# Attention probabilities turned in 32x32 squares by VectorE and exchanged through DRAM, in place of TensorE transposes

## The reference, cut to what matters

```
# layer 1
s = jnp.einsum('bhqe,bhke->bhqk', q, k) * scale
s = jnp.where(mask, s, jnp.finfo(s.dtype).min)
p = jax.nn.softmax(s, axis=-1)
o = jnp.einsum('bhqk,bhke->bhqe', p, v)
# layer 2
attn = jnp.einsum('bqc,bkc->bqk', q * scale, k)
attn = attn + rel_h[:, :, :, :, None] + rel_w[:, :, :, None, :]
attn = jax.nn.softmax(attn, axis=-1)
out = attn @ v
```

## Time and profile before

| | |
|---|---|
| median of 3 runs | 1289.74 us (1288.63 to 1292.06) |
| the profiled execution | 1289.51 us, span 1287.5 us |
| PE busy | 1256.3 us, 98% of the span |
| DVE / ACT / POOL busy | 631.2 / 537.7 / 641.0 us |
| mean granted TensorE clock | 0.998 of full speed |
| DMA | 96.33 MB, mean 75 GB/s |

### The profile page before, as it was taken

The page is one execution under the profiler, slowest core; times in us unless marked ns, Lnnn a source line. Parts: engine busy times, 40 slices in busy tenths (PEclk is TensorE's granted clock), DMA queues, the critical chain, the costliest instruction groups (busy, mean ns, idle before and its releaser), DMA issues.

```text
span 1287.5 us, 19996 instructions
## 1 busy us (share of the span) xinstructions
PE 1256.3 (98%) x7216; PEld 1018.3 (79%) x7216; DVE 631.2 (49%) x1323; ACT 537.7 (42%) x1357; POOL 641.0 (50%) x726
## 2 busy tenths in 40 slices
PE   6999998999999999999999999999999999999998
PEld 4887894478888888888888888888888887778787
DVE  7533453774444233545243465754436656666212
ACT  3612140045656430656452066564305665543212
POOL 4633299055454556555546655455565554564000
PEclk9999999999999999999999999999999999999999
DMA  5211123022222233222233323233333233220011
GB/s 179 86 44 42 43 55 103 8 70 75 67 82 67 81 80 95 74 75 75 74 81 97 97 81 95 80 90 86 91 91 93 82 93 81 73 74 1 17 50 66
DMA packets 83297, 96.33 MB, mean 75 GB/s; under 512 B 24960, under 2 KB 46112, under 8 KB 83200
## 3 DMA queue, kind: packets, MB, share of 16 engines
q1 hardware_dynamic: 82048, 92.97, 25.4%
q10 hardware_dynamic: 1152, 2.10, 0.5%
HBM read 82.45 MB, written 8.39 MB: 71 GB/s over the span
## 4 chain that ended last, share of the span: by engine, by line
PE 88%; DVE 5%; issue 2%; ACT 2%; SPq 1%; DMA 0%; POOL 0%; ACTq 0%; DVEq 0%; POOLq 0%
PE PS L1126 53%; PE PS L680 6%; PE PS L1762 5%; PE PS L1194 4%; PE PS L1171 4%; PE PS L945 3%; PE PS L1210 2%; PE PS L960 2%; PE PS L1220 2%; PE PS L1779 2%; PE PS L1240 1%; SPq L1027 1%; PE PS L663 1%; PE PS L954 1%; PE PS L1186 1%
## 5 line engine op out<-in xcount | busy, mean ns | idle before, releaser
L1126 PE MATMUL PS<-XB,w_hi 128*128 128x512 f32 x1024 | 358.3, 403 | 1.4 <-POOL w_lo L227 1.2
L225 POOL CAST w_hi<-w_raw 128x512 fp32r<-128x512 f32 x195 | 124.9, 640 | 327.6 <-PE PS L1126 254.8
L227 POOL TENSOR_TENSOR w_lo<-w_raw,w_hi 128x512 fp32r<-128x512 f32 x195 | 253.7, 1301 | 15.6
L1126 PEld LDWEIGHTS PS<-XB,w_hi 128*128 128x128 f32 x1024 | 192.3, 188 | 41.8 <-issue 2.4
L1126 PE MATMUL PS<-XB,w_lo 128*128 128x512 f32 x512 | 200.0, 391 | 0.0
L1126 PE MATMUL PS<-XB,part 128*128 128x512 f32 x768 | 198.9, 397 | 0.0
L1126 PEld LDWEIGHTS PS<-XB,part 128*128 128x128 f32 x768 | 140.1, 188 | 27.8
L1404 ACT ACTIVATE part<-PS,nmax 128x256 f32<-128x256 f32 (+1 forms) x256 | 112.4, 447 | 64.4 <-DVE nmax L1529 44.7
L1421 ACT ACTIVATE part<-PS 128x384 f32<-128x384 f32 (+1 forms) x128 | 69.6, 544 | 135.1 <-PE PS L1194 134.9
L225 POOL CAST part<-part 128x512 fp32r<-128x512 f32 x85 | 55.8, 656 | 122.3 <-PE PS L1126 121.6
L227 POOL TENSOR_TENSOR part<-part,part 128x512 fp32r<-128x512 f32 x85 | 111.2, 1308 | 6.8
(11 more groups left out here) (140 smaller groups left out, 1986.4 us busy)
## 6 DMA issues: line engine op xcount, KB each, us to landing
w_raw<-in_w SPq DMA_DIRECT2D x187, 256.0 KB, 2.7
part<-in_w SPq DMA_DIRECT2D x85, 256.0 KB, 2.7
strips<-part SPq DMA_DIRECT2D x16, 256.0 KB, 3.3
out_x<-xT SPq DMA_DIRECT2D x16, 256.0 KB, 2.1
part<-strips SPq DMA_DIRECT2D x128, 24.0 KB
xT<-in_x ACTq DMA_DIRECT2D x8, 256.0 KB, 7.6
xT<-in_x SPq DMA_DIRECT2D x8, 256.0 KB, 9.8
w_raw<-in_w SPq DMA_DIRECT2D x16, 128.0 KB, 3.4
```

The costliest lines, as they stand in the source:

```text
L225: pool.tensor_copy(hi, raw).then_inc(w_hi_done, 1)
L227: pool.tensor_tensor(lo, raw, hi.bitcast(F32), ALU.subtract).then_inc(w_ready, 1)
L1126: m = nc.tensor.matmul(PS[:, bank, :], wt[:, (c % 4) * P:(c % 4) * P + P], rhs(hl, c), start=c == k == 0, stop=c == CK - 1 and k == 2)
```

## The change

The PE transposes of probabilities and their copies by ACT go. DVE turns each tile of probabilities in 32x32 squares (`turn_probs`, now a VectorE function) into `probB`. The squares still have to change places among the four groups of 32 partitions: SP writes them to the DRAM tensor `turned` (four transfers for a batch a of an item, 128 pieces each) and reads them back into `probT` (one transfer for each a). `PROBS_AT` says behind which weight half block that is issued. `attend(i)` waits for the reads and stands behind `scores(i + 1)`; its right operand is read from the squares by a four-part pattern. Probabilities have two buffers instead of four, and score banks are free when the exponentials are taken.

Beside it: V's blocks are loaded ahead of the output blocks; Q goes to bank X, `turn_values` to a score bank; the strips are written from ACT's queue; K's scale of layer 2 is applied where relative positions are added, so K's evacuation has one DVE operation instead of two; the lambda part's shifts for t = 0 are issued by ACT, and its key groups are ordered so that those that need t = 0 come later; in layer 0 two of four evacuations of Q go ahead of the copies of windows; at the end the normalization of the last half is done in three portions around the evacuations of the first product.

```diff
             if i + 1 < ITEMS:
                 take_block(i + 1, "K")
+            take_block(i, "V", range(0 if i else 1, 2))
             if s and j == 0:
                 for o in range(CK):
                     take((s - 1, "O", o), STAGES[s - 1][0], "O", o)
-            take_block(i, "V", range(0 if i else 1, 2))
             if i + 2 < ITEMS:
...
         for jp in range(2):
             for b in (2 * jp, 2 * jp + 1):
                 exp_k(b)
+            evac_q(jp, range(2))
             if jp:
                 in_between()
-            evac_q(jp)
+            evac_q(jp, range(2, 4))
...
-    prob = carve(13824, [P, 4, 2, N])
+    prob = carve(13824, [P, 2, 2 * N])
+    probB = [carve(at, [P, 4 * N]) for at in (14848, 11264)]
...
-    probT = carve(16384, [P, 4, HALF])
+    probT = carve(16384, [P, 2, 4 * N])
+    turned = nc.dram_tensor("turned", (2, 2, P, 4 * N), F32).ap()
...
+    def add_keys_groups(b, mc):
+        groups.extend(("K", (b, mc, nh)) for nh in range(2))
+
+    def add_y_groups(b):
+        groups.extend(("Y", (b, nh, vt)) for nh in range(2) for vt in range(2))
+
+
+    KEYS = [(0, 1), (1, 1), (0, 0), (1, 0), (2, 1), (2, 0)]
+    for b, mc in KEYS:
+        add_keys_groups(b, mc)
+    add_y_groups(0)
+    for mc in (1, 0):
+        add_keys_groups(3, mc)
+    for b in range(1, B):
+        add_y_groups(b)
...
+    def shift(eng, t):
+        evacuated(eng, max(i for i, (kind, d) in enumerate(groups) if kind == "G" and d[0] == t))
+        for src, y, dst, mc in shifts(t):
+            eng.dma_start(A2[dst, mc, y, :, :].rearrange("p x g -> p (x g)"), G[t][src, y - rows_of[t][0], :])\
+                .then_inc(shifted[t], 16)
...
         copy_windows(act, range(2, len(quads)))
+        shift(act, 0)
...
-        for t in rows_of:
-            evacuated(sp, max(i for i, (kind, d) in enumerate(groups) if kind == "G" and d[0] == t))
-            for src, y, dst, mc in shifts(t):
-                sp.dma_start(A2[dst, mc, y, :, :].rearrange("p x g -> p (x g)"), G[t][src, y - rows_of[t][0], :])\
-                    .then_inc(shifted[t], 16)
+        for t in (3, 1, 2):
...
+    def squares(i):
+
+        return 4 if layer_of(i) == 2 else 3
+
+    def prob_at(i, qt):
+
+        return sum(hi - lo for lo, hi in spans(i)[:qt])
...
-                pe.wait_ge(t_evac, 4 * (i - 1) + 2 * a + 2)
+                pe.wait_ge(p_exp, 4 * (i - 1) + 2 * a + 2)
+                if a == 0 and turned_bank(i - 1) == S:
+                    pe.wait_ge(v_ready, i)
...
-        def turn_probs(i, k):
-
-            n = 4 * i + k
-            pe.wait_ge(p_norm, n + 1)
-            for kt_, qt, at in tiles(i):
-                m = nc.tensor.transpose(PS[:, S + k, at:at + P], prob[:, k, qt, kt_ * P:kt_ * P + P], ident[:, :])
-            m.then_inc(t_done, 1)
...
         def attend(i, a):
-            pe.wait_ge(t_evac, 4 * i + 2 * a + 2)
+            pe.wait_ge(p_in[a], 16 * (i + 1))
...
+            n = squares(i)
+
+            turned_p = probT[:, a, 0:8 * P * n // 4].rearrange("p (q h s j) -> p q h s j", q=4, h=2, s=n)
             if layer_of(i) == 2:
                 for kt_ in range(2):
                     for hh in range(2):
+                        rhs = turned_p[:, :, hh, kt_::2, :].rearrange("p q s j -> p s q j")
                         m = nc.tensor.matmul(PS[64 * hh:64 * hh + 64, O, a * N:a * N + N],
-                                             v[:, 2 * a + kt_, 64 * hh:64 * hh + 64],
...
-        def attention_block(i):
-
-            if i:
-                attend(i - 1, 0)
-                attend(i - 1, 1)
+        def score_block(i):
+
             scores(i, 0)
             scores(i, 1)
             relative(i + 1)
...
         for i in range(1, LAST - 1):
-            attention_block(i)
-            project(i + 1, "K", range(0, 6))
-            turn_probs(i, 0)
-            project(i + 1, "K", range(6, CK))
+            score_block(i)
+            attend(i - 1, 0)
+            attend(i - 1, 1)
+            project(i + 1, "K", range(CK))
+            project(i, "V", range(CK))
             if i % PAIRS == 0:
                 s = i // PAIRS - 1
                 out_block(s, 0, range(0, 2))
-                turn_probs(i, 1)
-                out_block(s, 0, range(2, 7))
-                turn_probs(i, 2)
-                out_block(s, 0, range(7, CK))
-                out_block(s, 1, range(0, 3))
-                turn_probs(i, 3)
-                out_block(s, 1, range(3, CK))
-                for o in range(2, CK):
+                turn_values(i)
+                out_block(s, 0, range(2, CK))
+                for o in range(1, CK):
                     out_block(s, o, range(CK))
-                project(i, "V", range(CK))
+                project(i + 2, "Q", range(CK))
+            else:
                 project(i + 2, "Q", range(0, 2))
                 turn_values(i)
                 project(i + 2, "Q", range(2, CK))
-            else:
-                project(i, "V", range(0, 2))
-                turn_probs(i, 1)
-                project(i, "V", range(2, 7))
-                turn_probs(i, 2)
-                project(i, "V", range(7, CK))
-                project(i + 2, "Q", range(0, 2))
-                turn_values(i)
-                project(i + 2, "Q", range(2, 3))
-                turn_probs(i, 3)
-                project(i + 2, "Q", range(3, CK))
...
+        attend(LAST, 0)
+        attend(LAST, 1)
+        for o in range(3):
+            out_block(3, o, range(7, CK))
+            for k in M_AFTER[o, 1]:
...
-            if n >= 4:
-                act.wait_ge(t_done, n - 3)
+            if n >= 2:
+                act.wait_ge(t_done, n - 1)
             for qt, (lo, hi) in enumerate(spans(i)):
-                last = nc.scalar.activation(prob[:, k, qt, lo:hi], PS[:, S + k, qt * N + lo:qt * N + hi],
+                at = prob_at(i, qt)
+                last = nc.scalar.activation(prob[:, n % 2, at:at + hi - lo], PS[:, S + k, qt * N + lo:qt * N + hi],
...
-        def evac_t(i, k):
-            n, w = 4 * i + k, P * len(tiles(i))
-            act.wait_ge(t_done, n + 1)
-            if i:
-                act.wait_ge(o_done, 2 * i)
-            nc.scalar.activation(probT[:, k, 0:w], PS[:, S + k, 0:w], ACT.Copy).then_inc(t_evac, 1)
...
+            strips_to_dram(act, i)
...
             exps(i, 0)
-            evac_relative(i + 1)
             exps(i, 1)
             normalize(i, 0)
             normalize(i, 1)
-            evac_t(i, 0)
+            evac_relative(i + 1)
             exps(i, 2)
             normalize(i, 2)
-            if i < LAST:
-                evac_k(i + 1)
-            else:
-                evac_v(i)
-            evac_t(i, 1)
             exps(i, 3)
+            if i and j == 0:
+                evac_o(i - 1)
             normalize(i, 3)
-            evac_t(i, 2)
-            out_between = i and i % PAIRS == 0
-            if i < LAST and not out_between:
-                evac_v(i)
-            evac_t(i, 3)
-            if out_between:
-                evac_v(i)
-            if 1 <= i % PAIRS <= 4:
-                for c in (2 * (i % PAIRS) - 2, 2 * (i % PAIRS) - 1):
-                    norm.y(nc.scalar, i // PAIRS + 1, c)
-                for c in (2 * (i % PAIRS) - 2, 2 * (i % PAIRS) - 1):
-                    norm.head(i // PAIRS + 1, c)
+            evac_k(i + 1)
+            if j:
+                evac_o(i - 1)
+            evac_v(i)
...
-                nc.vector.tensor_tensor(scores, scores, both_rel[:, n % 2, :, :, :].rearrange("p a h w -> p (a h w)"), ALU.add)\
-                    .then_inc(rel_added, 1)
+                nc.vector.scalar_tensor_tensor(scores, scores, SCALE, both_rel[:, n % 2, :, :, :].rearrange("p a h w -> p (a h w)"),
+                                               ALU.mult, ALU.add).then_inc(rel_added, 1)
...
+        def turn_probs(i, k):
+
+            n, a, hh, m = 4 * i + k, k // 2, k % 2, squares(i)
+            dve.wait_ge(p_norm, n + 1)
+            if i:
+                dve.wait_ge(p_out[a], 64 * i)
+            src = prob[:, n % 2, 0:P * m].rearrange("p (s b j) -> p b s j", s=m, b=4)
+            dst = probB[a][:, 0:2 * P * m].rearrange("p (b h s j) -> p b h s j", b=4, h=2, s=m)[:, :, hh, :, :]
+            nc.vector.transpose(dst, src).then_inc(t_done, 1)
...
             sum_relative(i, 0)
             sum_relative(i, 1)
             maxima(i, 0)
             maxima(i, 1)
             invert_sums(i, 0)
+            sum_relative(i, 2)
             invert_sums(i, 1)
-            if j:
-                rest_of_o(i - 1)
-            sum_relative(i, 2)
+            turn_probs(i, 0)
             maxima(i, 2)
+            turn_probs(i, 1)
             sum_relative(i, 3)
             invert_sums(i, 2)
             maxima(i, 3)
+            turn_probs(i, 2)
+            if i and j == 0:
+                rest_of_o(i - 1)
             invert_sums(i, 3)
+            turn_probs(i, 3)
             if i < LAST:
                 rest_of_k(i + 1)
```

(116 more changed lines are left out.)

188 lines of the change are left out of this document (80 added, 108 removed).

## The result

The changed kernel takes **1363.4 us** (median of 4 runs, 1359.0 to 1369.0) where the kernel before takes 1289.8 (4 runs on the same chip): ratio 1.057, 95% interval 1.053 to 1.061. It is slower; 1261 us was forecast, with a range up to 1290. The profiled execution took 1369.0, its span is 1367.1 us.

What follows compares the result with a forecast made beforehand. TensorE's stream was taken as the bound: 1289.5 - 50.6 (transposes) - 10.7 (waits removed elsewhere) + 32.7 (waits on the DRAM exchange) = 1260.9, so 1261 us. The forecast's own range was 1246 to 1279, the overall range 1232 to 1290.

Steps and rivals of the forecast that it cites:

- transposes gone: Attention items: 448 PE transposes of probabilities leave TensorE's stream, priced by starts at 0.115 and 0.1115 us each, 50.6 us gained.
- fixed parts: Layer 0, lambda part and last layer: waits of 1.8, 4.7 and 2.2 us go, plus 2 us of clock, 10.7 us gained.
- waits before attend: Attend waits for reads back from DRAM: 3.5 us once, 0.8 an item in layer 1, 1.5 in layer 2, 32.7 us added.
- clock: No cost in the sum for clock behind the new waits; a clock falling after each wait was listed as a sign of wrong.
- SP's schedule: SP's queue, timed from PE's end of V's first half: layer 1 writes 2.8 to 6.6 us, second read at 8.8; 0.47 per write.
- VectorE: Turning probabilities in squares on VectorE: 128 transposes, taken at 0.7 us each, which lies hidden.
- rival 3: VectorE's transposes take 1.9 us, turn_values waits some 1.5 us in 26 items, 25 us more: 1286 us; chance 0.13.
- Landings: Reads of turned probabilities from DRAM land in 3.1 us at 384 KB (layer 1) and 3.5 at 512 KB (layer 2).
- step (b): Lambda part: shift transfers for t = 0 go to ScalarE's queue, removing a 4.7 us wait and about 2 us of low clock.
- Rival 2: SP's queue becomes the bound, slower: 0.62 us per write and later landings, mean wait near 2.7 us, 1302 us; chance 0.11.
- The end, called "equal": After attend(31): a new 1.6 us wait for its evacuation, against three waits of about 1 us around the last transposes that go.
- rival 1: No wait is left before attend, as writes cost SP 0.37 us and reads land in 2.7, or with more slack: 1232 us; chance 0.17.

Runs made afterwards that it cites:

- both later: Changed kernel with attend(i-1) moved behind projection K(i+1) and GpSimd's inverse root (`power`) one half block later; 1251.3 us, 0.970 of the kernel before.
- not waited: Changed kernel with the DRAM exchange kept, but attend reads VectorE's squares before the exchange and waits only for VectorE's transposes; 1262.5 us, 0.978.
- one write of four: Changed kernel with only the first of four writes per batch kept in the exchange, in all items but 0, 1, 16 and 17; 1313.4 us, 1.018.
- fill run: Changed kernel with 5 unused matmuls added ahead of each half of attend in items 1 to 29; 1358.7 us, 1.054 of the kernel before.

## Why the prediction was wrong, step by step

| term of the sum | forecast | measured |
|---|---|---|
| transposes gone | -50.6 | 16 x 1.42 + 16 x 1.61 = -48.5 |
| fixed parts | -10.7 | -12.0 |
| waits before attend | +32.7 | 34.5 + 26.7 = +61.2 |
| V ahead of the output blocks | 0 | 4.36 + 4.36 + 4.43 = +13.1 |
| clock | 0 | at most 0.049 x 1367.1 - 0.002 x 1287.5 = +64 |

These give 1289.5 + 77.8 = 1367.3 of the 1369.0, but that closes too well. The clock's term, from mean clock and span, also counts the lower level where PE idled in it and lost nothing. By the trace's clock records the lower level lasted 134 us, with 19 us of idle PE among them; work at half the clock takes twice its time, so this cost (134 - 19) / 2 = 57, before the change 2. With +55 the sum is 1358, and some 10 us stay open. The same 10 us are open in "both later": 1289.5 - 60.5 + 2.8 of read waits + 7 for attend behind K + 1 of clock is 1240, its profiled execution took 1249.6. They lie at the stage turns and at the end (below).

- **Removed transposes: right.** The price by starts held to 4% in the sum, by the items with no wait in the run "not waited" (1.42 where 1.38 was forecast, 1.61 where 1.78 was); by duration it would have been 122 us. The Trainium skill's TensorE: Matmul & The Clock Gate, Part 4: PE-mode transpose, gives about 275 ns for one: that is what the record shows, and 2.4 times what one takes out of the stream here.
- **Fixed parts: right**, also in the clock of 1.00 at 205 to 226 us, where the earlier trace rows had 0.81.
- **SP's schedule: right.** In layer 1, V's first half ends 18 slots of 0.227 ahead of the turned values, which start at 338.54 in the turn below, so at 334.5. From there load +8 was forecast at 2.5, the last write's end at 6.6, the second read at 8.8; the timeline has 2.3, 6.6 and 8.9. It landed 4.1 us later (PE's second half of attend starts at 347.48) where 3.1 was taken. In layer 2, counted in the same way in the pass shown above, the gathers begin 2.7 us ahead of that point, so the first read goes at 8.3 where 9.5 was forecast. Its landing ate that: it is there at 13.1 (forecast 13.0), the second at 15.1 (14.3).

```profile
336.76 0.33 SPq L212 DMA_DIRECT2D part<-in_w  x1
337.19 3.93 SPq L1648 DMA_DIRECT2D turned<-part  x8
341.16 0.45 SPq L212 DMA_DIRECT2D w_raw<-in_w  x1
341.71 0.40 SPq L1655 DMA_DIRECT2D part<-turned  x1
342.99 0.33 SPq L212 DMA_DIRECT2D w_raw<-in_w  x1
343.42 0.38 SPq L1655 DMA_DIRECT2D part<-turned  x1
```

- **VectorE: right.** Its transposes take 0.64 us on the mean (0.7 taken), and rival 3 did not come.
- **Landings: a size that was off.** "3.1 at 384 KB, 3.5 at 512 KB" came from loads that stood nearly alone. These reads follow 768 KB or 1 MB of writes with weight loads among them. In the pass shown, the second read took 926.99 - 921.77 = 5.2 us; the 3.5 of the sum and the 3.2 of the formula quoted beside it are both well under that. The sum had 3.5 + 14 x 0.8 + 12 x 1.5; measured are 4.4 in item 1, 22.3 / 14 = 1.6 in layer 1, and 34.5 / 13 = 2.7 in the items of layer 2 that wait. The start was taken too short as well: item 2 still waits 3.7. With one write of four the landing is 4.4; what makes up the rest was not separated. The Trainium skill's DMA: Bandwidth & Descriptors, Latency and other measured facts, says that the latency to HBM grows with load. The trace agrees with the direction: the DMA share is 0.91 in the 7 us of the long landings.
- **Clock: the step that failed most.** The forecast priced a wait of 0.8 to 1.5 us at its own length, and named "a clock that falls after each wait" only as a thing that would prove it wrong, though its own step (b) had counted 2 us of clock behind one 4.7 us wait. Waits grown to 2 us and more an item are of the size at which, in the runs with added idle, the clock fell. The runs with added idle show that this needs no DMA, the fill run that work in its place prevents it. Priced by the records it is the largest term that the sum lacked, 55 us. With the waits as measured and nothing for clock and GpSimd the sum is 1289.5 - 60.5 + 61.2 = 1290: no gain, but no loss.
- **V ahead of the output blocks, taken as nothing: wrong.** What it costs was never asked. Behind the last output block now comes Q(i+2) at once, and `power` stands ahead of the split of its second half. The statistics of that block are 4.5 us late (last sum 517.64, power 522.17), while half of Q is 2.7 us of PE's work. This is the rule that the forecast used elsewhere: when a cover moves, name what it had hidden. That a later `power` cures it was shown; that V's old place alone would cure it as well was argued from the order and not tried.
- **The rivals.** Rival 2 (slower; decided at a mean of 2.2 us over 26 items) was right in sign, not in its reason. The measured mean is (61.2 - 4.4) / 26 = 2.2, just the point where the waits eat the gain; what made the kernel slower, clock and GpSimd, it lacked too. And it put the longer waits down to SP's price per write, which was near the forecast (0.49 and 0.55 for 0.47), where the landings made them.
- **The end, called "equal".** From scores(30) on 9.7 us were lost, 6.1 of them read waits. In "both later" the stretch is still 3 us over the kernel before, though transposes and a 2.2 us wait are gone from it. The waits there include 1.5 us for O's low part and 1.5 us for a matrix factor. The turns at items 8, 16 and 24 also come out no shorter than before, where each should be 1.4 to 1.8 us less. Both stay open, and with the 0.25 us that an item takes more with attend behind K they are why no version came to rival 1's 1232.

## What to carry to other kernels

Where the bounding engine's work is traded for a wait, price the wait by its length and by the clock behind it, from a row of the same trace that shows an idle of that size; a wait of 2 us here cost nearly twice its length in most items. A landing time read from a quiet stretch was too short here for a read behind a burst (3.5 against 5.1 us): ask what is issued in the 10 us ahead of it. If a round trip is late by a few us each turn, move its consumer past one block of independent work before giving it up: one moved line turned 5.7% slower into 1.5% faster, and with one more into 3% faster.

## What the runs showed of the hardware that was not expected

Adding 290 unused matmuls (83 us of recorded PE time) left the kernel's time no longer (1358.7 against 1363.4 us), because the clock stayed at 0.989 instead of 0.951. A single idle of 1.4 us cost no clock in most items, one of 2.0 us cost 1.6 us more than itself in nearly all (clock 0.66 over 5 us), and two waits of 1.20 and 0.85 us with 1.08 us of work between them cost about 3 us (0.58 over 7 us). DMA traffic at a share of 0.70 over an item did not lower the clock.
